# Another order of scores, transposes and weighted pieces in the wide blocks of an attention loop

## The chip, the cores and the metric

One NeuronCore of one Trainium2 chip runs the whole program. The metric is the device time of one execution in microseconds (us); the time before is the median of three executions.

## The reference, cut to what matters

One decoder layer on x (4 batches, 512 tokens, 128 features): layer norm and causal self attention with 16 heads of 8 features and a relative position term, then cross attention to 77 context tokens, then a mixture of 8 experts. The change is in the self attention:

```
q, k, v = split_heads(x @ Wq + bq), split_heads(x @ Wk + bk), split_heads(x @ Wv + bv)
scores = einsum('bhid,bhjd->bhij', q, k)
rel    = einsum('bhid,pd->bhip', q, rel_key)
bias   = take_along_axis(rel, clip(j - i + p - 1, 0, p - 1))
logits = where(j <= i, (scores + bias) * scale, -inf)
attn   = softmax(logits, axis=-1)
out    = einsum('bhij,bhjd->bhid', attn, v)
```

## The kernel before

A block g (0 to 15) is one tile of 128 queries of one batch. Batch g // 4 visits its tiles in the order ORDER = [2, 1, 3, 0]. Tile number blk sees blk * 128 whole keys and its own diagonal part, so the blocks with blk 2 and 3 (g even) are the wide ones. A block has 8 steps, u = 0 to 7, and s = 8 g + u counts steps. A step handles 16 queries and all 16 heads.

What a step needs, in the names used from here on (the number is the step u in the block, negative ones are of the block before):

- S(u), scores, on TensorE: 16 matmul instructions at L1403 (content) and 16 at L1413 (relative term), each on a 64x32 piece of the array, into one of two slots of psS. It waits until ScalarE has read step s - 2.
- max(u), L1058 on VectorE, and exp(u), L663 on ScalarE (two activations with their sums), which writes prob.
- T(u), transposes of prob with the 128x128 array, L1432, into the two banks of psT, one unit per bank: 6 transposes for blk 2, 8 for blk 3. T(u) waits for exp(u), and for each bank until the unit that was there has been copied out.
- cp(u), the copies out of psT: in wide blocks the first unit by VectorE (L1014), the second by ScalarE (L625).
- A(i), i = 0 to 3, the weighted pieces of the block before, L1372, on 128x32 pieces of the array: 8 instructions where that block was blk 0, 16 where it was blk 1.
- R, row sums of the block before (L1460), and Q, 128x128 pieces of later work (L1488, L1496, L1504), which exist in steps 1 to 3 of g = 6, 10, 14. P is an early probe (L1513) in step 6 of g = 10 and 14, O the output projection (L1379) in step 7.

Engines run their instructions in program order and meet through semaphores. TensorE's order is written out by hand: a step issues S(u), T(u-2), in steps 2 to 5 A(u-2), then whatever small pieces are due. ScalarE's order in a step is cp(u-2), exp(u), and in step 5 then the copy rec (L610, after R). VectorE's order in a step is: in step 2 two operations for the row sums, in step 6 `finish` (oT, L990, which waits for rec and for A(3)), then max(u), then cp(u-2), then pieces of other work: in g = 2 step 3 the four operations of head_scale, in g = 6, 10, 14 steps 4 to 7 pieces of a head norm, the last being L921. At step 7's scores_ready GpSimd starts to build the query blocks of the block after next (L479, L485).

```
            for s in range(ALL_STEPS):
                g, u = divmod(s, BS)
                scores(s)
                if s >= 2:
                    transpose_weights(s - 2)
                if g and 2 <= u <= 5:
                    attend_block(g - 1, u - 2)
```

Of the kernel before, what the change touches and what calls it, by code (L numbers as in the profile page):

```python
# [28 lines left out]
TB = S // T  # L29
# [31 lines left out]
def build(nc, x, ctx_in, pack_a, pack_b, rel_base, out):  # L61
# [6 lines left out]
    with ExitStack() as stack:  # L68
# [180 lines left out]
        ORDER = [TB - 2, 1, TB - 1, 0]  # L249
# [5 lines left out]
        def width(blk, u):  # L255


            return (blk * BS + (5 if u in (2, 3) else u + 1)) * QG

        def units(blk):  # L260


            return [list(range(j, min(j + 2, blk + 1))) for j in range(0, blk + 1, 2)]
# [40 lines left out]
        def tile_of(g):  # L304

            return g // TB * TB + ORDER[g % TB]
# [497 lines left out]
        def _(dve):  # L804
# [187 lines left out]
            def add_y(k, tile):  # L992

                dve.wait_ge(y_ready, k + 1)
                xt = X[:, bass.ds(tile, 1), :].rearrange("p o d -> p (o d)")
                v.tensor_tensor(xt, psM[:, T:2 * T], xt, ALU.add).then_inc(y_added, 1)
# [49 lines left out]
            for s in range(ALL_STEPS):  # L1046
                g, u = divmod(s, BS)
                wide = width(ORDER[g % TB], u)
                if g and u == 2:
                    spread_sums(g - 1)  # L1050
                if g and u == BS - 2:
                    finish(g - 1)
                if g == 2 and u == 0:
                    dve.wait_ge(bias_added, B)
                if g > 1 and u == 0:
                    add_y(g - 2, tile_of(g - 2))
                dve.wait_ge(scores_ready, s + 1)
                v.tensor_reduce(neg_max[:, s % 2], psS[:, 2 * (s % 2):2 * (s % 2) + 2, 0:wide],  # L1058
                                AX_X, ALU.max, negate=True).then_inc(max_ready, 1)
                if s >= 2:  # L1060
                    copy_units(s - 2)
                if s == KEYS_AT:
                    dve.wait_ge(ctx_k_copied, 1)
                    head_centre(ctx_k[:], xc_flat[0:M], sq_flat[0:M], stat[0:M], M, TB * H)
                if s == KEYS_SCALED:
                    dve.wait_ge(x_max_cleared, 2)
                    head_scale(xc_flat[0:M], stat[0:M], M, TB * H, B)

                b, n = divmod(g, TB)
                f = b - 1  # L1070
                if f >= 0 and n == 1 and u == 1:
                    dve.wait_ge(y_added, (f + 1) * TB + ONE)
                    ln_mean(f)
                if f >= 0 and n == 1 and u == 2:
                    ln_subtract(f)
                if f >= 0 and n == 1 and u == 3:
                    ln_square()
                if f >= 0 and n == 1 and u == 4:
                    ln_sum()
                if f >= 0 and n == 1 and u == 5:  # L1080
                    refine(stat, TB, B + 1 + 2 * f)
                    ln_multiply()
                if f >= 0 and n == 2 and u == 4:
                    dve.wait_ge(piece_read, piece_at(f, 3) + 1)
                    head_mean(stage_flat, stat, TB * H)
                if f >= 0 and n == 2 and u == 5:
                    head_subtract(stage_flat, xc_flat, stat, 128, TB * H)
                if f >= 0 and n == 2 and u == 6:
                    head_square(xc_flat, sq_flat)
                if f >= 0 and n == 2 and u == 7:  # L1090
                    head_sum(sq_flat, stat, TB * H)
                if f >= 1 and n == 0 and u == 4:
                    refine(stat, TB * H, B + 2 * f)
                if f >= 1 and n == 0 and u == 5:

                    dve.wait_ge(piece_ready, piece_at(f - 1, 0))
                    head_multiply(xc_flat, stat, 128)

                if (g, u) in EARLY_PROBES:
                    x_max_half(*divmod(EARLY_PROBES.index((g, u)), 2 * TB), psOM)  # L1100
                if (g, u) == EARLY_SHIFT:
                    x_shift(0, psO)
# [221 lines left out]
        def _(pe):  # L1324
# [62 lines left out]
            def scores(s):  # L1387

                g, u = divmod(s, BS)
                b, n = divmod(g, TB)  # L1390
                blk = ORDER[n]
                wide = width(blk, u)
                if u == 0:
                    pe.wait_ge(q_blk_ready, g + 1)
                    pe.wait_ge(q_rel_ready, g + 1)
                pe.wait_ge(scores_read, PRO + s - 1)


                for c in range(QG // QT):
                    q0 = QG * u + QT * c  # L1400
                    for half in range(2):
                        rows = slice(HALF_ROWS * half, HALF_ROWS * (half + 1))
                        mm(psS[32 * c:32 * c + 32, 2 * (s % 2) + half, 0:wide],  # L1403
                           q_blk[rows, g % 2, q0:q0 + QT, :].rearrange("p i h -> p (i h)"),
                           kT[rows, b * S:b * S + wide], start=True, stop=False)

                for c in range(QG // QT):
                    q0 = QG * u + QT * c
                    i0 = blk * T + q0
                    lo = max(0, i0 - P)  # L1410
                    for half in range(2):
                        rows = slice(HALF_ROWS * half, HALF_ROWS * half + QT * HD + QT)
                        ins = mm(psS[32 * c:32 * c + 32, 2 * (s % 2) + half, lo:wide],  # L1413
                                 q_rel[rows, g % 2, q0:q0 + QT, :].rearrange("p i h -> p (i h)"),
                                 rel[rows, lo - i0 + P:wide - i0 + P], start=False, stop=True)
                ins.then_inc(scores_ready, 1)

            def transpose_weights(s):

                g, u = divmod(s, BS)  # L1420
                blk = ORDER[g % TB]
                for i, js in enumerate(units(blk)):
                    if i == 0:
                        pe.wait_ge(scores_read, PRO + s + 1)
                    k = first_unit[g, u] + i

                    pe.wait_ge(psT_read[k % 2], PRO + k // 2)
                    for jn, j in enumerate(js):
                        w = T if j < blk else width(0, u)
                        for half in range(2):  # L1430
                            at = (jn * 2 + half) * T
                            ins = nc.tensor.transpose(psT[0:w, k % 2, at:at + T],  # L1432
                                                      prob[:, s % 4, half, j * T:j * T + w], ident)
                    ins.then_inc(psT_ready[k % 2], 1)
# [112 lines left out]

            for s in range(ALL_STEPS):
                g, u = divmod(s, BS)
                scores(s)  # L1550
                if s >= 2:
                    transpose_weights(s - 2)
                if g and 2 <= u <= 5:
                    attend_block(g - 1, u - 2)
                b, n = divmod(g, TB)
                f = b - 1
                if b == 0 and n == 3 and u in KEY_STEPS:
                    key_piece(KEY_STEPS.index(u), g)
                if (g, u) in EARLY_PROBES:
                    early_probe(g, u)  # L1560
                if (g, u) == EARLY_SHIFT:
                    pe.wait_ge(psO_read, PRO + g)
                    x_shift_of(0, psO)
                for f, i in pieces_of(g, u):
                    if u > 4:
                        pe.wait_ge(rec_copied, g)
                    else:
                        pe.wait_ge(y_added, g - 1 + ONE)
                    pe.wait_ge(x_probe_read, probes_until(g, u))
                    if i < 2:  # L1570
                        tokens_piece(f, i)
                    elif i < 4:
                        queries_piece(f, i - 2)
                    else:
                        heads_piece(f, i - 4)
                if g and u == 4:
                    pe.wait_ge(piece_read, pieces_until(g, u))
                    pe.wait_ge(x_probe_read, probes_until(g, u))
                    sum_rows(g - 1)
                if g and u == 7:  # L1580
                    pe.wait_ge(piece_read, pieces_until(g, u))
                    pe.wait_ge(x_probe_read, probes_until(g, u))
                    project_o(g - 1, cb["wo"])
# [317 lines left out]
```

## Time and profile before

| what | value |
|---|---|
| median of 3 executions | 498.36 us (495.96 to 498.57) |
| the profiled execution's own time | 497.16 us |
| its span | 495.4 us |
| TensorE busy | 449.7 us, 91% of the span |
| VectorE busy | 335.2 us, 68% |
| ScalarE busy | 267.2 us, 54% |
| GpSimd busy | 162.0 us, 33% |
| mean granted TensorE clock | 0.976 |

The span runs from the first to the last instruction; the execution's own time has 1.8 us more around it. Busy time of matmuls is modelled at its ends and overlaps, so the distance from one group's start to the next group's start is the better duration on TensorE.

### The profile page before, as it was taken

To read this page: it belongs to the slowest core of one execution; us is meant where nothing else is said; L and a number is where in the kernel's file an instruction comes from. 1 tells how busy PE (TensorE), PEld (TensorE's weight loads), DVE (VectorE), ACT (ScalarE), POOL (GpSimd) and SP (SyncE) were. 2 spreads that over 40 slices of the span, in tenths; PEclk is the share of its full clock that TensorE was granted. 3 is DMA by queue.
4 is the path that set the end of the run, shared out by engine and by line. 5 is a ranking of instruction groups with operands and counts; after the bars stand their busy time and mean duration, and the time that the engine had idled before them with its cause. 6 is when DMAs were issued, how large, how long until landed. Compare 5 with 4: busy or idle time off the path is not lost.

```text
span 495.4 us, 17255 instructions
## 1 busy us (share of the span) xinstructions
PE 449.7 (91%) x7304; PEld 274.2 (55%) x7304; DVE 335.2 (68%) x684; ACT 267.2 (54%) x811; POOL 162.0 (33%) x95
## 2 busy tenths in 40 slices
PE   0879999999999799999799999998898989999997
PEld 0554655655655555655565665564454434666765
DVE  5555886657977667885857887766667587466633
ACT  2546556756456446556535655554454556554653
POOL 7147383333350952360752422084300000001000
PEclk9999999999999799999889999999889899999999
DMA  8211000000100000000000000000000004503151
GB/s 287 66 70 46 26 3 24 24 18 8 26 24 1 24 10 17 26 24 2 24 3 24 3 3 3 3 4 2 2 0 1 1 0 172 171 23 141 53 176 38
DMA packets 17465, 19.49 MB, mean 39 GB/s; under 512 B 1659, under 2 KB 14575, under 8 KB 17263
## 3 DMA queue, kind: packets, MB, share of 16 engines
q1 hardware_dynamic: 17391, 18.41, 11.5%
q8 instruction: 58, 0.95, 0.8%
q14 instruction: 16, 0.13, 0.1%
HBM read 16.17 MB, written 2.16 MB: 37 GB/s over the span
## 4 chain that ended last, share of the span: by engine, by line
PE 70%; DVE 17%; issue 5%; ACT 5%; DMA 2%; POOL 1%; DVEq 0%; SPq 0%; ACTq 0%; POOLq 0%
PE psT L1432 15%; PE psS L1403 14%; PE psS L1413 8%; PE psOM L1372 8%; PE psT L1792 5%; PE psS L1775 4%; DVE neg_max L1058 3%; DVE x_max L1033 2%; PE psS L1622 2%; PE psOM L1513 2%; ACT prob L663 2%; PE psT L1513 2%; PE psOM L1649 1%; DVE prob L1278 1%; PE psOM L1460 1%
## 5 line engine op out<-in xcount | busy, mean ns | idle before, releaser
L663 ACT ACTIVATE prob<-psS,neg_max 128x208 f32<-128x208 f32 (+23 forms) x256 | 121.2, 479 | 74.3 <-DVE neg_max L1058 74.1
L1058 DVE TENSOR_REDUCE neg_max<-psS 128x2 f32<-128x672 f32 (+23 forms) x128 | 91.7, 717 | 64.8 <-PE psS L1413 63.8
L445 POOL TENSOR_TENSOR stat<-stat,pack_a_sb 128x4 f32<-128x4 f32 (+2 forms) x16 | 54.7, 3416 | 169.9 <-DVE stat L876 123.0
L1432 PE MATMUL psT<-pack_a_sb,prob 128*128 128x128 f32 (+4 forms) x640 | 99.2, 287 | 6.3 <-DVE pt_even L1014 3.3
L1432 PEld LDWEIGHTS psT<-pack_a_sb,prob 128*128 128x128 f32 (+4 forms) x640 | 65.1, 133 | 48.5 <-issue 31.4
L1403 PE MATMUL psS<-k_v,q_both 64*32 64x336 f32 (+23 forms) x2048 | 88.5, 403 | 2.6 <-ACT prob L663 1.3
L1413 PE MATMUL psS<-rel_shifted,q_both 36*32 36x268 f32 (+16 forms) x2048 | 71.8, 338 | 0.0
L479 POOL TENSOR_TENSOR q_both<-qT,pack_a_sb 128x1024 f32<-128x1024 f32 x16 | 31.6, 1973 | 85.4 <-PE psS L1413 82.9
L1413 PEld LDWEIGHTS psS<-rel_shifted,q_both 36*32 36x32 f32 x2048 | 37.4, 110 | 24.7 <-issue 17.5
L663 ACT ACTIVATION_READ_ACCUMULATOR prob<-psS,neg_max 128x1 f32 x256 | 50.5, 197 | 0.0
L1792 PEld LDWEIGHTS psT<-pack_b_sb,prob 128*128 128x128 f32 x288 | 36.1, 191 | 18.6 <-DVE prob L1278 11.7
L1014 DVE COPY pt_even<-psT 128x512 f32<-128x512 f32 x64 | 43.6, 682 | 3.4 <-PE psT L1432 3.2
L713 ACT ACTIVATE prob<-psS 77x2048 f32<-77x2048 f32 x16 | 29.9, 1872 | 22.4 <-PE psS L1622 22.4
L1792 PE MATMUL psT<-pack_b_sb,prob 128*128 128x128 f32 x288 | 38.7, 278 | 3.6 <-DVE prob L1278 3.6
L485 POOL TENSOR_TENSOR q_both<-q_rep,pack_a_sb 128x1024 f32<-128x1024 f32 x16 | 41.1, 2568 | 0.0
L1403 PEld LDWEIGHTS psS<-k_v,q_both 64*32 64x32 f32 x2048 | 23.6, 106 | 25.3 <-issue 17.8
L1775 PE MATMUL psS<-qT,pack_b_sb 128*128 128x512 f32 x72 | 36.4, 594 | 0.0
L625 ACT ACTIVATE pt_diag<-psT 80x256 f32<-80x256 f32 (+2 forms) x64 | 23.9, 374 | 23.0 <-PE psT L1432 23.0
L625 ACT ACTIVATE pt_even<-psT 128x256 f32<-128x256 f32 x32 | 12.3, 383 | 33.4 <-PE psT L1432 33.4
L768 ACT ACTIVATE prob<-psS 128x512 f32<-128x512 f32 x36 | 21.2, 590 | 12.2 <-PE psS L1775 12.2
L1014 DVE COPY pt_diag<-psT 80x256 f32<-80x256 f32 (+2 forms) x64 | 26.3, 411 | 0.8 <-PE psT L1432 0.7
L1372 PE MATMUL psOM<-pt_diag,V_now 128*32 128x128 f32 x512 | 26.0, 280 | 0.0
(172 smaller groups left out, 597.7 us busy)
## 6 DMA issues: line engine op xcount, KB each, us to landing
q_rep<-q_scratch SPq DMA_DIRECT2D x128, 32.0 KB
k_v<-w_scratch SPq DMA_DIRECT2D x8, 512.0 KB, 5.9
q_both<-w_scratch SPq DMA_DIRECT2D x8, 512.0 KB, 6.6
pack_b_sb<-pack_b_dram SPq DMA_DIRECT2D x1, 1641.5 KB, 9.7
X<-x_dram SPq DMA_DIRECT2D x4, 256.0 KB, 5.3
q_scratch<-qT SPq DMA_DIRECT2D x4, 256.0 KB, 2.0
out_dram<-X SPq DMA_DIRECT2D x4, 256.0 KB, 2.3
pack_a_sb<-pack_a_dram SPq DMA_DIRECT2D x1, 535.0 KB, 4.4
```

What stands on the lines that cost most here:

```text
L445: nc.gpsimd.tensor_tensor(st[:, 5, 0:groups], st[:, 2, 0:groups], ca["root"][0:parts, 0:groups], ALU.pow).then_inc(seeded, 1)
L485: nc.gpsimd.tensor_tensor(q_rel[:, slot].rearrange("p (g i) h -> p g i h", i=QT), q_rep[:, slot].rearrange("p h (g i) -> p g i h", i=QT), ...
L625: ins = nc.scalar.activation(dst, src, ACT.Copy)
L663: ins = nc.scalar.activation(prob[:, s % 4, half, 0:wide], psS[:, 2 * (s % 2) + half, 0:wide], ACT.Exp, bias=neg_max[:, s % 2, half:half + 1],
L1014: ins = v.tensor_copy(dst, src)
L1058: v.tensor_reduce(neg_max[:, s % 2], psS[:, 2 * (s % 2):2 * (s % 2) + 2, 0:wide], AX_X, ALU.max, negate=True).then_inc(max_ready, 1)
L1372: ins = mm(psO[quadrant * 32:quadrant * 32 + 32, 0:T], val, w, start=(i == 0 and n == 0), stop=(i == HQ - 1 and n == len(mine[0]) - 1))
L1403: mm(psS[32 * c:32 * c + 32, 2 * (s % 2) + half, 0:wide], q_blk[rows, g % 2, q0:q0 + QT, :].rearrange("p i h -> p (i h)"), kT[rows, b * S: ...
L1413: ins = mm(psS[32 * c:32 * c + 32, 2 * (s % 2) + half, lo:wide], q_rel[rows, g % 2, q0:q0 + QT, :].rearrange("p i h -> p (i h)"), rel[rows ...
L1432: ins = nc.tensor.transpose(psT[0:w, k % 2, at:at + T], prob[:, s % 4, half, j * T:j * T + w], ident)
L1775: mm(psS[:, k % 4, :], cb["w1"][:, e * D:e * D + D], xn_of[b], start=True, stop=True).then_inc(h_ready, 1)
L1792: ins = mm(psT[:, b % 2, t * D:t * D + D], hidden[:, k % 3, t * T:t * T + T], cb["w2"][:, e * D:e * D + D], start=(i == 0 and t == 0), sto ...
```

## The change

In the wide blocks other than the first one (g = 2, 4, ... 14, seven blocks) steps 2 to 5 get another order. TensorE issues S2 T0 A0 A1 (Q) T1 S3 (Q) S4 T2 A2 A3 R T3 S5, and goes on with S6 T4 S7 T5 as before; before it was S2 T0 A0 (Q) S3 T1 A1 (Q) S4 T2 A2 R S5 T3 A3. In steps 3 and 5 VectorE does cp(u-2) ahead of max(u). No instruction is added or removed on any engine, no DMA is moved, and no wait has another value.

```
+        def mirrored(g, u):
+            return g > 0 and ORDER[g % TB] >= 2 and 2 <= u <= 5
...
+                if mirrored(g, u) and u % 2:
+                    copy_units(s - 2)
                 dve.wait_ge(scores_ready, s + 1)
                 v.tensor_reduce(neg_max[:, s % 2], psS[:, 2 * (s % 2):2 * (s % 2) + 2, 0:wide],
                                 AX_X, ALU.max, negate=True).then_inc(max_ready, 1)
-                if s >= 2:
+                if s >= 2 and not (mirrored(g, u) and u % 2):
                     copy_units(s - 2)
...
-                scores(s)
-                if s >= 2:
-                    transpose_weights(s - 2)
-                if g and 2 <= u <= 5:
-                    attend_block(g - 1, u - 2)
+                if mirrored(g, u):
+                    if u % 2:
+                        transpose_weights(s - 2)
+                        scores(s)
+                    else:
+                        scores(s)
+                        transpose_weights(s - 2)
+                        attend_block(g - 1, u - 2)
+                        attend_block(g - 1, u - 1)
+                else:
+                    scores(s)
+                    if s >= 2:
+                        transpose_weights(s - 2)
+                    if g and 2 <= u <= 5:
+                        attend_block(g - 1, u - 2)
```

## Rows read from the trace of the kernel before

**Rows 1.** The page's part 1, busy time, share and instructions of each engine.

```profile
PE 449.7 (91%) x7304; PEld 274.2 (55%) x7304; DVE 335.2 (68%) x684; ACT 267.2 (54%) x811; POOL 162.0 (33%) x95
```

**Rows 2.** The page's part 4, the chain that ended last, by engine.

```profile
PE 70%; DVE 17%; issue 5%; ACT 5%; DMA 2%; POOL 1%; DVEq 0%; SPq 0%; ACTq 0%; POOLq 0%
```

**Rows 3.** Windows, PE alone, g = 4 from S2 to S7: length, busy, clock.

```profile
107.76:119.58 11.82, 11.82 (x227) 1.00 0.09 25
```

**Rows 4.** Timeline of g = 4, PE, steps 3 and 4: start, duration, instruction.

```profile
110.14 0.80 PE L1403 MATMUL psS<-k_v,q_both 64*32 64x336 f32 x16
...
111.34 0.87 PE L1432 MATMUL psT<-pack_a_sb,prob 128*128 128x128 f32 x6
112.14 0.42 PE L1372 MATMUL psOM<-pt_diag,V_now 128*32 128x128 f32 x8
112.50 0.80 PE L1403 MATMUL psS<-k_v,q_both 64*32 64x336 f32 x16
```

**Rows 5.** Timeline after the loop, PE: four weighted pieces in a row, then R.

```profile
339.64 1.08 PE L1372 MATMUL psOM<-pt_diag,V_now 128*32 128x128 f32 x32
340.65 0.44 PE L1460 MATMUL psOM<-spread,pack_a_sb 128*64 128x128 f32 x4
```

**Rows 6.** Timeline of g = 4, DVE, step 2: cp(0).

```profile
109.95 0.68 DVE L1014 COPY pt_even<-psT 128x512 f32<-128x512 f32 x1
```

**Rows 7.** Timeline of g = 7, step 0: a copy, and the transposes that waited for it.

```profile
161.96 0.68 DVE L1014 COPY pt_even<-psT 128x512 f32<-128x512 f32 x1
...
162.79 1.07 PE L1432 MATMUL psT<-pack_a_sb,prob 128*128 128x128 f32 x8 [0.80 <-DVE pt_even L1014]
```

**Rows 8.** Timeline of g = 4, all engines, from S5 to T5.

```profile
115.19 0.82 PE L1403 MATMUL psS<-k_v,q_both 64*32 64x352 f32 x16
...
116.39 0.87 PE L1432 MATMUL psT<-pack_a_sb,prob 128*128 128x128 f32 x6
116.58 0.89 DVE L1058 TENSOR_REDUCE neg_max<-psS 128x2 f32<-128x704 f32 x1 [1.27 <-PE psS L1413]
...
117.58 0.54 ACT L663 ACTIVATE prob<-psS,neg_max 128x352 f32<-128x352 f32 x1
...
118.64 0.27 ACT L610 ACTIVATE rec<-psOM 128x128 f32<-128x128 f32 x1
...
118.94 0.29 DVE L990 TENSOR_TENSOR oT<-psOM,rec 128x128 f32<-128x128 f32 x1 [0.86 <-ACT rec L610]
119.15 0.91 DVE L1058 TENSOR_REDUCE neg_max<-psS 128x2 f32<-128x736 f32 x1
...
119.58 0.88 PE L1403 MATMUL psS<-k_v,q_both 64*32 64x384 f32 x16
...
120.82 0.87 PE L1432 MATMUL psT<-pack_a_sb,prob 128*128 128x128 f32 x6
```

**Rows 9.** Timeline of g = 2, DVE, steps 3 and 4: head_scale's first operation, max(4).

```profile
78.56 0.21 DVE L834 SCALAR_TENSOR_TENSOR stat<-stat 77x64 f32<-77x64 f32 x1
...
79.93 1.11 DVE L1058 TENSOR_REDUCE neg_max<-psS 128x2 f32<-128x928 f32 x1
```

**Rows 10.** Timeline of g = 6: T3, max(5), S7, and the end of the head norm.

```profile
154.90 1.09 PE L1432 MATMUL psT<-pack_a_sb,prob 128*128 128x128 f32 x8
155.16 1.16 DVE L1058 TENSOR_REDUCE neg_max<-psS 128x2 f32<-128x960 f32 x1 [0.90 <-PE psS L1413]
...
158.95 1.09 PE L1403 MATMUL psS<-k_v,q_both 64*32 64x512 f32 x16
...
162.58 2.55 POOL L485 TENSOR_TENSOR q_both<-q_rep,pack_a_sb 128x1024 f32<-128x1024 f32 x1
...
163.27 1.92 DVE L921 TENSOR_SCALAR stat<-stat 128x64 f32<-128x64 f32 x1
```

**Rows 11.** Windows of all engines from 158 to 178 (g = 7): PE's busy time, clock.

```profile
158.00:178.00 20.00, 16.88 (x422) 11.79 (x430) 12.26 (x24) 9.62 (x42) 15.02 (x3) 0.83 0.06 16
```

**Rows 12.** Timeline of g = 14, PE, step 6: the early probe.

```profile
317.96 0.80 PE L1513 MATMUL psOM<-x_key,x_qT 32*128 32x154 f32 x8
```

## The prediction, on record before the changed kernel was built

> **What bounds the kernel now.** I read the page first: TensorE is busy 91% of the span, VectorE 68%, ScalarE 54% [rows 1], and the chain that ended last lies on TensorE for 70% and on VectorE for 17% [rows 2]. Then the windows view: from S2 to S7 of block g = 4 TensorE is busy all 11.82 us at the full clock, 2.4 GHz [rows 3]. So inside a wide block the order of TensorE's instructions sets the time, and the other engines keep up. Then the timeline of such a block, to see by how much they keep up. That is the question here, since the change adds no work and removes none: it only moves S5 and its relatives.
>
> **What the new order saves on TensorE.** In step 3 S takes 1.20 us (110.14 to 111.34), T 0.80, A 0.36 [rows 4]. Four pieces A of the same size in a row took 1.01 us (339.64 to 340.65) and not 4 x 0.36 = 1.44 [rows 5], so each A that follows an A saves (1.44 - 1.01) / 3 = 0.14 us: a change from one shape of the array to another costs about that. The new order puts A1 behind A0, A3 behind A2, S4 behind S3 and S6 behind S5. For S behind S no row exists. Below nothing is excluded, since the instructions are the same ones; the bounds are 0 and the 0.14 of A, and I take 0.12. For T behind A (before, T always stood behind S) I take the same 0.80, with 0.14 either way. A wide block saves 2 x 0.14 + 2 x 0.12 = 0.52 us. In g = 6, 10, 14 a Q stands between S3 and S4, but another comes to stand before T1, with the same array shape: again about 0.5. Seven blocks give 3.6 us.
>
> The Trainium skill says the same (TensorEngine Tiling, Key Properties): changing the tiling mode drains TensorE. Rows 4 and 5 agree, at 0.14 us a change; by that rule alone the kernel would be faster, which is the first rival below.
>
> **What the order costs: T1 behind T0.** A bank of psT must be copied before the next unit goes in. cp(0) runs from 109.95 to 110.63 [rows 6], and transposes start 0.15 us after the copy they wait for (162.64 to 162.79) [rows 7]. Before, A0 and S3 lay between T0 and T1. Now only A0 and A1 do: A0 starts at 110.14 - 0.36 = 109.78, and with A1 (0.22) TensorE is ready for T1 at 110.36. T1 starts at 110.78 instead: 0.4 us lost in g = 4, 8, 12. Nothing behind T1 on TensorE can pass it. In g = 2 and 6 T and A are longer and I count 0.0 to 0.2. VectorE's copy ahead of the maximum costs nothing of its own: in steps 3 and 5 T(u-2) now precedes S(u), and VectorE waits for S(u) anyway.
>
> **What the order costs: the end of S5.** From T1's start at 110.78: T1, T2, T3 2.40, S3 and S4 1.20 + 1.17 - 0.12 = 2.25, A2 and A3 0.58, R 0.36 (the 0.36 from A's end to S5 before, like A), S5 1.20 (115.19 to 116.39). That is 6.79, and S5 ends at 117.57, not at 116.39 [rows 8]: 1.18 later, because T3 and A3 now stand ahead of it. Behind it come only S6 and T4 before S7, where T3, A3, S6 and T4 stood (116.39 to 119.58 = 3.19, so S6 and T4 2.03). Everything that hangs on S5 has lost that cover:
>
> - max(5) starts 0.19 after S5's end, 117.76, and ends at 118.65. exp(5) follows; rec started 1.17 after max(5)'s end (117.47 to 118.64), now 119.82. S7 needs exp(5), since it overwrites its slot: it starts at about 119.9, where TensorE is ready at 117.57 - 0.12 + 2.03 = 119.48 and where it started at 119.58. S7 comes 0.3 us later.
> - VectorE's `finish` waits for rec, which ScalarE runs behind exp(5), and max(6) and cp(4) are queued behind `finish`. max(6) started 1.68 after max(5)'s end (117.47 to 119.15) [rows 8], now 120.33, though S6 has been done since about 118.7. Then 0.91 for max(6), 0.6 for cp(4), 0.15 for the semaphore: T5 can start at 121.98, where it started at 120.82. T5, O and the next block's S0 are 1.16 later.
>
> A few tenths come back in the short steps of the next block, whose T waited before too. I take +1.0 us for each of g = 4, 8, 12, with the 0.5 saved already inside.
>
> **g = 2.** The same chain with longer operations, and head_scale on VectorE: 78.56 to 79.93 is 1.37 us in step 3 [rows 9], ahead of max(4) and cp(2). Before, T1, A1 and S4 covered it. T3 now stands where S5 stood. From S3's end: max(3) until 1.4, head_scale until 2.8, max(4) 1.11, cp(2) 0.6, semaphore 0.15, so T3 may start at 4.65. TensorE has S4, T2, A2, A3, R, about 3.7 (T 1.02, S 1.38, A 0.57 + 0.43, R 0.37). Stall 0.9, against 0.2 less at T1: 1.0 + 0.9 - 0.2 = 1.7 us.
>
> **g = 6, 10, 14.** From T3's start to S7 before is 4.05 (154.90 to 158.95) [rows 10]. S5's end comes about 1.1 later; from it, max(5) starts after 0.3, takes 1.16 [rows 10], and exp(5), with 480 columns for 352, about 1.45: 2.95 to S7. So S7 moves by 1.1 + 2.95 - 4.05 = 0.0, say 0.0 to 0.3. T5 and T6 are about 1.0 later through `finish`, but that is absorbed: L921, the last of the head norm, takes 1.92 us and ends at 165.19, with GpSimd's L485 at 165.13 [rows 10], and VectorE goes on to the next block only then. GpSimd starts from S7's end. So g = 6 loses 0.2. In g = 10 and 14 the probe P stands ahead of S7 and waits for `finish` (317.96) [rows 12], which comes about 1.0 later, while TensorE is ready 0.4 later or so: 0.6 each.
>
> **Sum.** 1.7 + 3 x 1.0 + 0.2 + 2 x 0.6 = +6.1 us. Against the profiled execution (span 495.4, own time 497.16) this gives 503.3. That execution lies 1.2 under the median of 498.36, and of the 6.1 some tenths may come back around g = 7 and 11, where TensorE stands and waits already; I predict 503.8. A measurement of this kernel can tell about 0.5%, 2.5 us, from no change.
>
> **The rivals.**
>
> 1. The array changes decide. If S7, T5 and T1 found their inputs in time, the block would keep its 0.5 us: 498.4 - 3.6 = 494.8. For it: TensorE is the bound [rows 1 to 3] and the 0.14 is measured. Against it: exp(5) starts from S5's end and no row leaves room. It decides only if the chain S5's end to T5 is under 3.2 us; the rows give 4.4. Chance 0.07.
> 2. Gain and loss cancel: the stalls are absorbed at each block's start, where the narrow steps wait anyway. In g = 7 TensorE is busy 16.88 of 20 us [rows 11]. If the three blocks after g = 4, 8, 12 absorb their 1.0 as well, 1.7 + 1.4 is left less what merging S saves more, 498 to 500.5. Against it: the blocks with blk 1 are nearly full. Chance 0.13.
> 3. The clock. In the stretch from 158 to 178 the granted clock is 0.83 [rows 11], so part of it ran at 1.2 GHz, after TensorE had stood still at T6 [rows 7]. The change adds 1 us of standing at the end of g = 4, 8, 12 and of g = 2. If some of these fall to the lower level, or the stretches at g = 7 and 11 grow, each costs 1 to 2 us: 506 to 509. For it: the new waits lie close together. Against it: other narrow blocks with waits kept 2.4 GHz. Chance 0.14.
>
> The forecast itself, 501 to 506, has 0.66.
>
> **How the numbers follow.** The forecast's own range comes from the bounds: S behind S at 0 (+1.7) or 0.14 (-0.3), T behind A (2 in each block, so 14 x 0.14 = 2.0 either way), 0.0 to 0.3 in S7 of g = 6, 10, 14. Where a wait ends last, a dearer T is half hidden, so I take 501 to 506 for it. To hold 8 in 10 the range takes most of rival 2 and half of rival 3: 499.0 to 507.5. Faster by over 0.5%: 0.07. Within: most of rival 2 and the foot of the forecast, 0.13. Slower: 0.80.
>
> **What would show it.** In the trace after: A0 to T1 in g = 4 0.58 us plus a wait for pt_even of about 0.4; S4 starting 1.1 after S3; max(5) starting 1.2 later; L990 and max(6) 1.2 later, with the wait for rec; T5 with 1.2 of idle time behind cp(4); S7 with 0.3 behind exp(5). In g = 2 T3 idle 0.9 behind a copy. TensorE's busy sum falls by a few us while the span grows. The prediction is wrong if T5 starts right behind S7, or if S behind S saves far more than 0.14.

## The result, and the profile after

The changed kernel takes 502.55 us (median of 5 executions, 501.06 to 503.04), the kernel before 498.36. From all executions timed side by side the ratio is 1.0095, 95% interval 1.0059 to 1.0132 (the two medians alone give 1.0084). It is slower by about 1%. 503.8 was predicted, with slower at 0.80.

The page of the changed kernel's profile, parts 1 and 4, and its dearest line, which answer to [rows 1, 2]:

```profile
span 501.2 us, 17255 instructions
...
PE 443.6 (89%) x7304; PEld 274.3 (55%) x7304; DVE 336.4 (67%) x684; ACT 268.0 (53%) x811; POOL 161.6 (32%) x95
...
PE 63%; DVE 22%; ACT 6%; issue 6%; DMA 2%; POOL 1%; DVEq 0%; SPq 0%; ACTq 0%; POOLq 0%
...
L668 ACT ACTIVATE prob<-psS,neg_max 128x208 f32<-128x208 f32 (+23 forms) x256 | 121.5, 480 | 107.5 <-DVE neg_max L1065 107.5
```

TensorE is busy 6.1 us less (449.7 to 443.6) while the span grows by 5.8: it does the same work in less time and waits more. Not all of the 6.1 is the order's. The mean granted clock is 0.983 for 0.976, which is about 17 us of the span at 1.2 GHz for 24; the 7 us between them, at half the clock, make my estimate of its share up to 3.5 us. The chain that ended last has moved from TensorE (70% to 63%) to VectorE (17% to 22%). ScalarE's exp now waits 107.5 us for a maximum, where it was 74.1. The waits view says for whom TensorE itself waits (engine and line, for whom; us in total, times, longest):

```profile
PE psT L1439 <- DVE pt_even L1019: 9.9, 15, 2.3
...
PE psS L1410 <- ACT prob L668: 3.1, 7, 1.1
```

The same two waits before:

```profile
PE psT L1432 <- DVE pt_even L1014: 3.3, 5, 0.8
...
PE psS L1403 <- ACT prob L663: 1.3, 2, 1.1
```

The transposes wait 6.6 us more for a copy and the scores 1.8 us more for an exp, 8.4 us together. The two savings come off that, so the loss is less than the waits.

The timeline of g = 4 from S2's transposes on, changed kernel (start, duration, instruction; in brackets the idle time before it and what ended it), which answers to [rows 4, 6, 8]:

```profile
112.49 0.88 PE L1439 MATMUL psT<-pack_a_sb,prob 128*128 128x128 f32 x6
...
113.30 0.64 PE L1379 MATMUL psOM<-pt_diag,V_now 128*32 128x128 f32 x16
113.46 0.68 DVE L1019 COPY pt_even<-psT 128x512 f32<-128x512 f32 x1
...
114.28 0.85 PE L1439 MATMUL psT<-pack_a_sb,prob 128*128 128x128 f32 x6 [0.34 <-DVE pt_even L1019]
...
115.06 0.80 PE L1410 MATMUL psS<-k_v,q_both 64*32 64x336 f32 x16
...
116.14 0.75 PE L1410 MATMUL psS<-k_v,q_both 64*32 64x336 f32 x16
...
117.27 0.87 PE L1439 MATMUL psT<-pack_a_sb,prob 128*128 128x128 f32 x6
...
118.07 0.64 PE L1379 MATMUL psOM<-pt_diag,V_now 128*32 128x128 f32 x16
...
118.64 0.44 PE L1467 MATMUL psOM<-spread,pack_a_sb 128*64 128x128 f32 x4
...
119.86 0.82 PE L1410 MATMUL psS<-k_v,q_both 64*32 64x352 f32 x16
...
120.93 0.81 PE L1410 MATMUL psS<-k_v,q_both 64*32 64x368 f32 x16
121.25 0.89 DVE L1065 TENSOR_REDUCE neg_max<-psS 128x2 f32<-128x704 f32 x1 [0.81 <-PE psS L1420]
...
122.17 0.55 ACT L668 ACTIVATE prob<-psS,neg_max 128x352 f32<-128x352 f32 x1 [1.83 <-DVE neg_max L1065]
...
123.25 0.28 ACT L615 ACTIVATE rec<-psOM 128x128 f32<-128x128 f32 x1
...
123.41 0.88 PE L1410 MATMUL psS<-k_v,q_both 64*32 64x384 f32 x16 [0.42 <-ACT prob L668]
123.55 0.29 DVE L995 TENSOR_TENSOR oT<-psOM,rec 128x128 f32<-128x128 f32 x1 [1.42 <-ACT rec L615]
123.76 0.91 DVE L1065 TENSOR_REDUCE neg_max<-psS 128x2 f32<-128x736 f32 x1
...
124.59 0.68 DVE L1019 COPY pt_even<-psT 128x512 f32<-128x512 f32 x1
...
125.42 0.84 PE L1439 MATMUL psT<-pack_a_sb,prob 128*128 128x128 f32 x6 [0.69 <-DVE pt_even L1019]
```

Read it as three waits. T1 (114.28) waits for cp(0), which ends at 114.14. S7 (123.41) waits 0.42 for exp(5), which could start only at 122.17. T5 (125.42) waits 0.69 for cp(4), at the end of the chain S5, max(5), exp(5), rec, oT, max(6), cp(4). And two savings: S3 and S4 together take 2.21 (115.06 to 117.27, where T2 starts), for 1.20 + 1.17 = 2.37 before, and a pair of A takes 0.57 (A2 at 118.07, R at 118.64), for 2 x 0.36 = 0.72.

To see where the 5.8 us went I took the start of S2 of each block in both traces (the first matmul of L1403 and of L1410) and the change of their difference from one block to the next:

| stretch | changed minus before, us | predicted |
|---|---|---|
| up to the first S0 | +2.1 | 0 |
| g = 2 | +1.5 | +1.7 |
| g = 4, 8, 12 | +0.9, +1.1, +1.1 | +1.0 each |
| g = 6 | +0.8 | +0.2 |
| g = 7 | -1.3 | 0 |
| g = 10, 14 | +0.4, +0.9 | +0.6 each |
| other narrow blocks, together | 0.0 | 0 |
| after the last S7 | -1.6 | 0 |

The loop alone, from the first S0 to the last S7, is 5.3 us slower, where 6.1 was predicted. The 2.1 ahead of it is not the change, and most of it is the clock. The windows view of the two executions (stretch, its us, busy time and count of PE, PEld, DVE, ACT and POOL, granted clock, DMA share, GB/s), the changed kernel first:

```profile
28.00:31.40 3.40, 3.40 (x12) 2.37 (x11) 1.90 (x6) 1.57 (x7) 1.01 (x1) 0.50 0.21 77
171.40:174.80 3.40, 3.17 (x46) 2.23 (x50) 1.81 (x6) 1.73 (x12) 3.40 (x1) 0.50 0.25 68
```

And the kernel before:

```profile
28.00:31.40 3.40, 3.39 (x28) 2.92 (x27) 2.08 (x7) 1.31 (x5) 1.21 (x2) 1.00 0.21 77
```

At 28 us both kernels do the same projections, and only one of these two executions ran them at 1.2 GHz. The traces of the experiments below bear it out: in the four kernels with 3.4 us at 1.2 GHz at 26 to 28 us (this one among them) the first S0 is 1.7 to 2.1 us later than before, in the other seven 0.0 to 0.5, whichever order they have.

In g = 7 the changed kernel's stretch at the lower level is 3.4 us long (171.4 to 174.8), the one before had 6.8 (165.8 to 172.6) [rows 11]; that gave 1.3 us back. One kernel below, with steps 2 and 3 in the new order and A2 A3 in step 5, has the 6.8 us at the same place, and its g = 7 shifts by 0.0. Behind the loop the kernel before had three stretches of 3.4 us at 1.2 GHz and the changed one had one, which fits the -1.6.

### The profile page after: what moved, and what is told of

Read it like the earlier page. It is cut to its first block, busy times and chain, and to the rows that moved or that the text cites. A ratio compares the mean times of both kernels' runs of the same rounds, so it can differ in the third digit from the quotient of the medians.

```text
span 501.2 us, 17255 instructions
## 1 busy us (share of the span) xinstructions
PE 443.6 (89%) x7304; PEld 274.3 (55%) x7304; DVE 336.4 (67%) x684; ACT 268.0 (53%) x811; POOL 161.6 (32%) x95
## 4 chain that ended last, share of the span: by engine, by line
PE 63%; DVE 22%; ACT 6%; issue 6%; DMA 2%; POOL 1%; DVEq 0%; SPq 0%; ACTq 0%; POOLq 0%
PE psT L1439 13%; PE psS L1410 12%; PE psS L1420 7%; PE psOM L1379 7%; DVE neg_max L1065 6%; PE psT L1809 5%; PE psS L1792 4%; ACT prob L668 3%; DVE x_max L1038 2%; PE psT L1520 2%; DVE pt_even L1019 2%; PE psOM L1520 2%; PE psS L1639 1%; PE psOM L1666 1%; DVE prob L1285 1%
## 5 line engine op out<-in xcount | busy, mean ns | idle before, releaser
L668 ACT ACTIVATE prob<-psS,neg_max 128x208 f32<-128x208 f32 (+23 forms) x256 | 121.5, 480 | 107.5 <-DVE neg_max L1065 107.5
L450 POOL TENSOR_TENSOR stat<-stat,pack_a_sb 128x4 f32<-128x4 f32 (+2 forms) x16 | 54.7, 3417 | 171.4 <-DVE stat L881 122.9
L1410 PE MATMUL psS<-k_v,q_both 64*32 64x336 f32 (+23 forms) x2048 | 87.9, 401 | 4.3 <-ACT prob L668 3.1
L1420 PE MATMUL psS<-rel_shifted,q_both 36*32 36x272 f32 (+17 forms) x2048 | 71.4, 338 | 0.0
L484 POOL TENSOR_TENSOR q_both<-qT,pack_a_sb 128x1024 f32<-128x1024 f32 x16 | 31.6, 1974 | 97.5 <-PE psS L1420 93.4
L490 POOL TENSOR_TENSOR q_both<-q_rep,pack_a_sb 128x1024 f32<-128x1024 f32 x16 | 41.5, 2593 | 0.0
L1410 PEld LDWEIGHTS psS<-k_v,q_both 64*32 64x32 f32 x2048 | 24.7, 105 | 27.2 <-issue 13.9
L1379 PE MATMUL psOM<-pt_even,V_now 128*32 128x128 f32 x640 | 24.8, 283 | 0.4 <-DVE x_max L1038 0.4
L1379 PE MATMUL psOM<-pt_diag,V_now 128*32 128x128 f32 x512 | 24.5, 276 | 0.0
```

Of the source, the lines that this page charges most:

```text
L450: nc.gpsimd.tensor_tensor(st[:, 5, 0:groups], st[:, 2, 0:groups], ca["root"][0:parts, 0:groups], ALU.pow).then_inc(seeded, 1)
L484: nc.gpsimd.tensor_tensor(q_blk[:, slot], qT[:, bass.ds(b * S + blk * T, T)].unsqueeze(2).to_broadcast([128, T, HH]), ca["half_mask"].unsq ...
L490: nc.gpsimd.tensor_tensor(q_rel[:, slot].rearrange("p (g i) h -> p g i h", i=QT), q_rep[:, slot].rearrange("p h (g i) -> p g i h", i=QT), ...
L668: ins = nc.scalar.activation(prob[:, s % 4, half, 0:wide], psS[:, 2 * (s % 2) + half, 0:wide], ACT.Exp, bias=neg_max[:, s % 2, half:half + 1],
L1379: ins = mm(psO[quadrant * 32:quadrant * 32 + 32, 0:T], val, w, start=(i == 0 and n == 0), stop=(i == HQ - 1 and n == len(mine[0]) - 1))
L1410: mm(psS[32 * c:32 * c + 32, 2 * (s % 2) + half, 0:wide], q_blk[rows, g % 2, q0:q0 + QT, :].rearrange("p i h -> p (i h)"), kT[rows, b * S: ...
```

## The experiments

In their traces "loop" is the change of the time from the first S0 to the last S7 against the trace of before, and block shifts are from S2 to S2 as above. A ratio is to the kernel before, timed beside it, whose median was 498.74 us beside the first four experiments, 497.33 beside the next four and 497.52 beside the last two.

**Rec ahead of exp(5).** The changed kernel, with this on ScalarE:

```
+                if g and u == 5:
+                    copy_inverses(g - 1)
                 act.wait_ge(max_ready, s + 1)
...
                 ins.then_inc(scores_read, 1)
-                if g and u == 5:
-                    copy_inverses(g - 1)
```

> The changed kernel, with ScalarE's copy rec (after R) ahead of exp(5) and no longer behind it, in every block. My theory (two waits behind the late S5: S7 for exp(5), and max(6), cp(4), T5 for finish, which waits for rec): finish can run before max(5) has ended, max(6) starts right after S6, and the idle time ahead of T5 in g = 4, 8, 12 (0.69 us in g = 4 of the changed kernel) goes; S7's wait of 0.4 stays. The loop, 5.35 us slower than before in the changed kernel's trace, is then 1 to 2.5 us slower than before; the median falls by 3 to 4 us against the changed kernel, to 498.5 to 500. Rival (what costs is T1 behind cp(0) and T3 behind cp(2), and the clock): under 1 us falls away.

Measured: 499.37 us, ratio 1.0007 (0.9976 to 1.0038), loop +0.9. Most of the loss is gone: over the seven wide blocks the trace is 1.8 us behind the kernel before, where the changed kernel is 6.7. Its timeline in g = 4:

```profile
117.72 0.26 ACT L615 ACTIVATE rec<-psOM 128x128 f32<-128x128 f32 x1
...
119.53 0.28 DVE L995 TENSOR_TENSOR oT<-psOM,rec 128x128 f32<-128x128 f32 x1
...
119.80 0.93 DVE L1065 TENSOR_REDUCE neg_max<-psS 128x2 f32<-128x736 f32 x1
...
120.88 0.88 PE L1410 MATMUL psS<-k_v,q_both 64*32 64x384 f32 x16 [0.42 <-ACT prob L670]
...
122.13 0.87 PE L1439 MATMUL psT<-pack_a_sb,prob 128*128 128x128 f32 x6
```

Max(6) starts 0.2 after S6's end, T5 has no wait, and S7's 0.42 is still there. g = 4, 8, 12 now lose 0.3, 0.2, 0.2 (0.9, 1.1, 1.1 without). The `finish` branch was the larger of the two that hang on S5, and the late exp(5) by itself the smaller.

**Only steps 2 and 3 in the new order.**

```
-            return g > 0 and ORDER[g % TB] >= 2 and 2 <= u <= 5
+            return g > 0 and ORDER[g % TB] >= 2 and 2 <= u <= 3
```

> Only steps 2 and 3 of the wide blocks get the new order; steps 4 to 7 are as before (S4 T2 A2 R S5 T3 A3). My theory: S5 keeps its cover, so no wait at S7, T5 or P. The block has the wait of T1 (0.34 us in g = 4) and the saving of one A behind A and one S behind S (0.15 + 0.11). That is +0.1 in g = 4, 8, 12 and between -0.3 and 0.1 in g = 2, 6, 10, 14: the kernel within 1 us of the one before. Rival (T1's wait is what costs): +2 us or more.

Measured: 497.42 us, ratio 0.9966 (0.9941 to 0.9992), loop -0.7; g = 4, 8, 12 +0.1 each, g = 2 -0.2. T1's wait of 0.35 to 0.4 costs about what the two savings bring (0.14 + 0.16), and not more. The rival that T1's wait carries the loss is out.

**Only steps 4 and 5 in the new order** (the same line with 4 <= u <= 5).

> Only steps 4 and 5 of the wide blocks get the new order (S4 T2 A2 A3 R T3 S5 S6). My theory: the whole loss through S5 stays (S7 0.3 to 0.4 behind exp(5), T5 0.7 to 1.2 behind finish, max(6), cp(4)), and T3's wait in g = 2, while T1's wait and half of the saving are gone. Loop 4.5 to 6 us slower than before. Rival (T1's wait and loss of cover in step 3 carry it): under 2 us slower.

Measured: 504.5 us, ratio 1.0118 (1.0087 to 1.0149), loop +5.1; g = 4, 8, 12 +0.8, +1.0, +1.0. Nearly the whole loss is in this half (6.5 us over the seven wide blocks, for 6.7), with the two waits of g = 4 as they were:

```profile
121.05 0.88 PE L1410 MATMUL psS<-k_v,q_both 64*32 64x384 f32 x16 [0.42 <-ACT prob L668]
...
123.07 0.84 PE L1439 MATMUL psT<-pack_a_sb,prob 128*128 128x128 f32 x6 [0.69 <-DVE pt_even L1019]
```

One detail did not come as stated. T3's wait in g = 2 was to stay, and it is gone: with S4 back behind T1 and A1, head_scale on VectorE is covered again, and T3 starts straight behind R (82.21 to 82.58). So g = 2 loses 0.9 and not 1.5; that wait needs both halves of the new order.

**VectorE's old order under TensorE's new one.**

```
-                if mirrored(g, u) and u % 2:
-                    copy_units(s - 2)
...
-                if s >= 2 and not (mirrored(g, u) and u % 2):
+                if s >= 2:
```

> The changed kernel with VectorE's order as it was before: max(u) ahead of cp(u-2) in steps 3 and 5 too. TensorE's order stays the new one. My theory: the copies ahead of the maximum cost nothing; without them cp(1) stands behind max(3), and T2 may just be late; cp(3) stands behind max(5), and in front of it finish and max(6) come no earlier, so that T4, which needs cp(3), is late by up to 1.5 us: T4 follows S6 at S5's end + 1.1, and cp(3) would end at S5's end + 0.3 + 0.9 + 0.6 = 1.8, so T4 waits 0.8 (blk 2) to 1.0 (blk 3). S7 waits for exp(5) anyway (0.4), so 0.4 to 0.6 a block is lost: 2.5 to 4 us slower than the changed kernel. Rival (the copies ahead delay the maximum and are part of the loss): faster than the changed kernel.

Measured: 508.04 us, ratio 1.0176 (1.0118 to 1.0235), loop +9.4, so 4.1 us behind the changed kernel's loop. The copies ahead of the maximum are no part of the loss; without them T2 and T4 wait as well (PE, g = 4):

```profile
116.99 0.84 PE L1437 MATMUL psT<-pack_a_sb,prob 128*128 128x128 f32 x6 [0.72 <-DVE pt_even L1019]
...
122.54 0.84 PE L1437 MATMUL psT<-pack_a_sb,prob 128*128 128x128 f32 x6 [0.70 <-DVE pt_even L1019]
```

T4's wait had been expected, T2's only as "may just be late", and it is as large. So the total is at the top of the expectation by the loop (4.1 for 2.5 to 4) and above it by the medians (508.04 against 502.55, 5.5).

**head_scale in step 4** (KEYS_SCALED = 20 for 19, in the changed kernel).

> The changed kernel with head_scale (four operations of VectorE, 1.37 us, once, in g = 2) in step 4 behind cp(2), and no longer in step 3 ahead of max(4). My theory: T3's wait in g = 2, worked out as 0.9 us, goes, and g = 2 loses 0.6 to 0.9 us less than in the changed kernel's trace (1.49), the other blocks are as they were. Rival (that wait belongs to exp(3) or to the order as such): g = 2 stays at 1.5.

The block shift of g = 2 is +0.7, for +1.5: 0.8 less, as expected. T3 in g = 2, in the changed kernel and then in this one:

```profile
84.90 1.06 PE L1439 MATMUL psT<-pack_a_sb,prob 128*128 128x128 f32 x8 [0.76 <-DVE pt_even L1019]
```

The timeline with head_scale in step 4:

```profile
83.64 1.09 PE L1439 MATMUL psT<-pack_a_sb,prob 128*128 128x128 f32 x8
```

The one execution took 505.94 us all the same, and most of it is accounted for: it had a stretch at 1.2 GHz that no other trace here has, in g = 14 and 15, which shifted by 2.5 and 0.9 us where the changed kernel had 0.9 and 0.0:

```profile
331.20:338.00 6.80, 6.80 (x124) 4.97 (x128) 3.56 (x8) 2.25 (x13) 6.80 (x1) 0.50 0.01 2
```

**Pairs of A alone.** Here the kernel before is changed, not the changed kernel:

```
-                if g and 2 <= u <= 5:
+                if g and ORDER[g % TB] >= 2 and u in (3, 5):
+                    attend_block(g - 1, u - 3)
+                    attend_block(g - 1, u - 2)
+                elif g and ORDER[g % TB] < 2 and 2 <= u <= 5:
                     attend_block(g - 1, u - 2)
```

> The kernel before, in which only the pieces A are paired in the wide blocks: S2 T0 S3 T1 A0 A1 (Q) S4 T2 R S5 T3 A2 A3 S6. S keeps its distance, T0 and T1 have S3 between them, and S5 keeps T3, A2, A3, S6, T4 ahead of S7. My theory (the saving of a changed array shape is real, and was lost only through the late S5 and T1): 2 x 0.15 us in each of 14 wide blocks but the first, that is seven blocks here: loop 2.1 us faster than before, median 496 to 497 beside 498.5. Rival (TensorE's saving comes out as a wait elsewhere whatever the order): within 0.5 us of the kernel before.

Measured: 493.69 us, ratio 0.9919 (0.989 to 0.9949), loop -2.5. Faster than both kernels. g = 4, 8, 12 gain 0.27, 0.28, 0.27, twice 0.14. No new wait stands in g = 4; its first pair:

```profile
111.87 0.64 PE L1372 MATMUL psOM<-pt_diag,V_now 128*32 128x128 f32 x16
112.45 0.80 PE L1403 MATMUL psS<-k_v,q_both 64*32 64x336 f32 x16
```

The median moved by 3.6 us (497.33 to 493.69), more than the loop's 2.5 in its one trace. In that trace the part ahead of the loop is 0.5 us longer and the part behind it 1.3 shorter, with one stretch of 3.4 us at 1.2 GHz fewer there; the rest is the difference between one execution and the median.

**Pairs alone, and rec ahead of exp(5)** (the two edits above together).

> The kernel with pairs alone, and rec ahead of exp(5) on ScalarE in every block. My theory: with S5 in its old place, finish is only 0.2 us late (max(6) started 0.38 after S6's end in g = 4 and 0.48 in g = 6 instead of 0.2), so an early rec moves max(6) up by 0.1 to 0.3 and shortens only the wait of T6 in g = 3, 7, 11, 15 (0.58 to 0.80): at most 1 us faster than pairs alone in all, about 0.5. Rival (rec's place is worth about the same in any order): 3 us faster than pairs alone, as between the changed kernel and that one with an early rec (3.2 us of the median).

Measured: 494.33 us, ratio 0.9946 (0.9914 to 0.9978): the same as pairs alone. Its loop is -4.1, but the 1.6 between the two traces lies in g = 6, 7, 10 and 11, around the stretches at the lower clock; in g = 2, 3, 4, 5, 8, 9, 12 and 14 they agree to 0.01 us. An early rec is worth something only where S5 is late.

**Steps 2 and 3 in the new order, A2 A3 together in step 5.** The edit is 2 <= u <= 3 as above, and this:

```
                     if s >= 2:
                         transpose_weights(s - 2)
-                    if g and 2 <= u <= 5:
+                    if g and ORDER[g % TB] >= 2:
+                        if u == 5:
+                            attend_block(g - 1, 2)
+                            attend_block(g - 1, 3)
+                    elif g and 2 <= u <= 5:
                         attend_block(g - 1, u - 2)
```

> Steps 2 and 3 in the new order, and A2 A3 together in step 5: S2 T0 A0 A1 T1 S3 S4 T2 R S5 T3 A2 A3 S6. My theory: as steps 2 and 3 alone (loop 0.74 us faster than before in its trace) and 0.15 us less for A3 behind A2 in each of seven blocks: loop 1.8 us faster than before. It should come out within 0.5 us of the kernel with pairs alone. Rival: T2, now straight in front of R and S5, moves S5 up and exp(3) is not there in time for S5, so no gain over steps 2 and 3 alone.

Measured: 497.19 us, ratio 1.0 (0.9977 to 1.0024), loop -1.0, g = 4, 8, 12 +0.1 each. A miss: 0.15 us a block was to come on top of steps 2 and 3 alone. In the timeline of g = 4 the row of R (L1467) stands ahead of S5, the row of exp(3)'s last read is at 116.94, and the idle time in brackets is that of S5's weight load (PEld):

```profile
116.71 0.44 PE L1467 MATMUL psOM<-spread,pack_a_sb 128*64 128x128 f32 x4
...
116.94 0.20 ACT L668 ACTIVATION_READ_ACCUMULATOR prob<-psS,neg_max 128x1 f32 x1
...
117.19 0.19 PEld L1410 LDWEIGHTS psS<-k_v,q_both 64*32 64x32 f32 x16 [0.28 <-ACT prob L668]
117.19 0.83 PE L1410 MATMUL psS<-k_v,q_both 64*32 64x352 f32 x16
```

S5 has come up to exp(3), as the rival said: exp(3) ends at 117.14 and S5's weights are loaded at 117.19. The end of R's row (116.71 + 0.44 = 117.15) hides it, since ends are modelled; from start to start R took 0.48 us here, for 0.37 with steps 2 and 3 alone and 0.36 before. That is 0.11 of the 0.14 that the second pair saves: from S4 to S6 this kernel takes 4.99 us and the one with steps 2 and 3 alone 5.01. The rival was right. In g = 2, which lost 0.1 and not gained, T3 waits 0.20 behind cp(2) as well (84.92).

**All four A in step 5 of the wide blocks** (as pairs alone, with `u == 5` and i = 0 to 3).

> As pairs alone, but all four A together in step 5 of the wide blocks: S2 T0 S3 T1 (Q) S4 T2 R S5 T3 A0 A1 A2 A3 S6. My theory (the saving is 0.15 us for each A behind an A, and nothing is lost as long as each exp has its cover): 3 x 0.15 us a block, loop about 3.1 us faster than before, 1 us faster than pairs alone. What could take it: S4 and S5 come 0.6 to 1.0 us earlier and S5 needs exp(3); from S3's end max(3) and exp(3) take 0.2 + 0.86 + 0.05 + 1.15 = 2.3 us in blk 2 while S4 and T2 take 2.0 and R 0.36, so S5 would wait by up to 0.1; in blk 3 2.8 against 2.8. Rival (those waits eat it, as in steps 2 and 3 with a pair behind): no faster than pairs alone.

Measured: 492.59 us, ratio 0.9884 (0.9857 to 0.991), loop -5.4; g = 4, 8, 12 gain 0.41 each, three times 0.14, and no wait of exp(3) came up. The fastest kernel of the study, though its interval overlaps that of pairs alone (0.9857 to 0.991, 0.989 to 0.9949). Of the loop's -5.4, g = 7 and 11 hold -1.7, where the stretches at the lower clock lie, so probably not the order's. Four A in one go:

```profile
117.49 1.08 PE L1372 MATMUL psOM<-pt_diag,V_now 128*32 128x128 f32 x32
118.50 0.85 PE L1403 MATMUL psS<-k_v,q_both 64*32 64x368 f32 x16
```

**Pairs in every block.**

> As pairs alone, but pairs (A0 A1 in step 3, A2 A3 in step 5) in every block, the narrow ones too. In the narrow blocks each A is what covers the chain S, max, exp: without A in steps 2 and 4 a T waits for its exp. My theory: in blocks with blk 0 and 1 S and T are short (S 0.4 to 0.9 us), so two S are closer together than the chain max and exp takes, and the 0.15 x 2 x 8 = 2.4 us is mostly lost or more than lost: between 1 us faster and 4 us slower than pairs alone. Rival: TensorE is the bound there too, 2.4 us faster.

The edit is the one of pairs alone with the first condition for all g. Measured: 494.57 us, ratio 0.9932 (0.9906 to 0.9957), loop -4.1: not to be told from pairs alone. g = 5, 9 and 13 are unchanged to 0.01 us, so there a saved array change is waited away, as expected. But g = 1 gains 0.4 and g = 15 0.7, and g = 2, which has the order of pairs alone, comes out 1.4 us worse than there (+1.1 for -0.3). There a small operation of VectorE met GpSimd's L479. With pairs alone it starts 0.23 us ahead of L479 and takes 0.42 (first two rows); here it starts 0.16 behind it and takes 2.08, and cp(0) and T1 come late behind it (last three rows):

```profile
74.18 0.42 DVE L1021 TENSOR_TENSOR spread<-row_inv,pack_a_sb 128x256 f32<-128x256 f32 x1
...
74.41 2.02 POOL L479 TENSOR_TENSOR q_both<-qT,pack_a_sb 128x1024 f32<-128x1024 f32 x1
...
73.16 1.97 POOL L479 TENSOR_TENSOR q_both<-qT,pack_a_sb 128x1024 f32<-128x1024 f32 x1
73.32 2.08 DVE L1021 TENSOR_TENSOR spread<-row_inv,pack_a_sb 128x256 f32<-128x256 f32 x1
...
77.18 1.06 PE L1432 MATMUL psT<-pack_a_sb,prob 128*128 128x128 f32 x8 [1.35 <-DVE pt_even L1014]
```

So the pairs in the narrow blocks did have a price here, by way of an engine that no edit touched.

## Why the prediction was right

**The saving.** Right in kind and size. A behind A saves 0.14 us (0.27 or 0.28 for two in a block, 0.41 for three in a row). S behind S saves 0.16 in g = 4 (2.21 for 2.37), for 0.12, and just above the 0.14 that was taken as the bound. T behind A or R costs what T behind S did, 0.78 for 0.80.

**T1 behind T0.** 0.4 was predicted for g = 4; from A1's end, 113.30 + 0.58 = 113.88, to 114.28 is 0.40.

**The end of S5.** Right, and it is the cause: with S5 in its old place (steps 2 and 3 alone, pairs, four A) the loss is gone, and with only steps 4 and 5 changed it is nearly whole. From S2's end to S7 and T5 the trace has 10.92 and 12.93 us; before, they were 10.60 and 11.84, so S7 is late by 0.3 and T5 by 1.1, for 0.3 and 1.16 predicted. Of the two branches, `finish` behind rec behind exp(5) carried most: an early rec took 4.4 of the loop's 5.3 us, or 4.9 of the 6.7 in the wide blocks.

**g = 2.** 1.5 for 1.7; head_scale's share is 0.8 by its own experiment, for 0.9. T1 has no wait there, where 0.0 to 0.2 was allowed for.

**g = 6, 10, 14.** Their sum, 2.1, is above the 1.4 predicted, and the reasoning on g = 6 failed: "that is absorbed: L921, the last of the head norm, takes 1.92 us and ends ... with GpSimd's L485". The 1.92 was not the operation's own length: in g = 14 of the same trace L921 takes 0.19 us, and the long one ended 0.06 behind GpSimd's L485. So what VectorE loses there depends on what it has at hand when GpSimd starts, and the change moved that. In the changed kernel another operation of VectorE was caught beside GpSimd's work, ahead of max(7), not behind it (g = 6, line 921 here is the square, L916 before):

```profile
165.15 1.97 POOL L484 TENSOR_TENSOR q_both<-qT,pack_a_sb 128x1024 f32<-128x1024 f32 x1 [15.86 <-PE psS L1420]
165.55 2.11 DVE L921 TENSOR_TENSOR sq<-xc 128x512 f32<-128x512 f32 x1
...
167.70 1.22 DVE L1065 TENSOR_REDUCE neg_max<-psS 128x2 f32<-128x1024 f32 x1
...
169.67 1.07 PE L1439 MATMUL psT<-pack_a_sb,prob 128*128 128x128 f32 x8 [2.33 <-DVE pt_even L1019]
```

So max(7), cp(5) and T6 came late with it. In g = 14 the probe P waited for oT as predicted (325.02, 1.02 of idle time), and that block lost 0.9 for 0.6.

**The sum.** 5.3 in the loop for 6.1, and the closeness is in part luck. The wide blocks lost 6.7, 0.6 more than forecast, most of it in g = 6; g = 7 gave 1.3 back, since its stretch at 1.2 GHz was half as long; the forecast had only some tenths there, and for another reason. That the span came out 5.8 longer is in part an accident of two other stretches, +2.1 ahead of the loop and -1.6 behind it. The median moved by 4.2 us, where 503.8 against 498.36 is 5.4: 1.2 less than forecast, well inside the spread of either kernel's executions.

**The rivals.** The first (TensorE's saving decides) needed the chain from S5's end to T5 to be under 3.2 us. It took 4.5 (120.93 to 125.42), but the saving itself is there to be had: an order that leaves S5 alone is faster than before. The second (absorbed in the narrow blocks) did not happen: g = 5, 9 and 13 gave back 0.0. Its range was also low for its own terms, since 1.7 + 1.4 on 498.4 is 501.5, and only an unnamed further saving brings that to 498 to 500.5. The third (more of the lower clock) was wrong for this trace, which has less of it; one execution of another kernel had such a stretch, worth 2.5 us in g = 14 and 15.

What stays open: why the clock's stretches at g = 7 and 11 are 3.4 us in some traces and 6.8 or 10.2 in others. No run separated it from the order of the instructions, but the order is not all: 27 executions of the kernel before had mean granted clocks from 0.962 to 0.983, with spans from 500.5 down to 493.7 us.

## What to carry to other kernels

When an order is mirrored to save changes between kinds of work, list for each producer what lay between it and its last consumer before and after; here two S in a row cut what TensorE had to do between S5 and S7 from 3.2 us to 2.1. Look past the direct consumer: the dearer branch was a small copy queued behind exp on ScalarE, whose reader stood at the head of VectorE's queue. And take the part of the saving that moves no producer: pairing or bundling A gave 0.8 to 1.2%.

## What the runs showed of the hardware

TensorE's granted clock differs between executions in stretches of a few us in which the work is the same (1.00 and 0.50 at 28 us above). One and the same kernel (before, 27 executions) had spans of 493.7 us at a mean of 0.983 and 500.5 at 0.962. Of the stretches, the one of 6.8 us in g = 14 and 15 cost 2.5 us against the changed kernel (2.5 + 0.9 for 0.9 + 0.0), though one edit lies between the two. A traced difference of 1 or 2 us between two kernels has to be located before it is believed.

An operation of VectorE on 128x512 elements took 2.11 us in g = 6 while GpSimd's L484 ran, and its neighbour of the same size 0.68 us at 161.88, with GpSimd idle. The long one ended at 167.66, 0.54 behind L484's end (167.12), as if it had stood still until then. The Trainium skill (SBUF — State Buffer, section "SBUF: two separate sides") says that a VectorE operation with two inputs in SBUF and a GpSimd operation that reads SBUF hold a shared pair of ports exclusively, the later one waiting for the whole of the earlier. The times agree, and L490 behind it took 3.00 us for 2.57 in g = 4. L1021 above, also with two inputs in SBUF, agrees too: started ahead of GpSimd's L479 it took 0.42 us, started behind it 2.08, and then it ended 0.27 behind L479's end. No run tried the ports by themselves. The profile counts such standing as busy time of VectorE, not as a wait. The short one of the two:

```profile
161.88 0.68 DVE L917 TENSOR_TENSOR xc<-stage,stat 128x512 f32<-128x512 f32 x1
```
